# Token dispatch in a state-space and mixture-of-experts kernel: counts by a masked scan and two matmuls, two expert blocks begun ahead of the last count, the second block table in four parts

## The reference

```python
gate_logits = einsum('bsd,ed->bse', x, gate_w) + gate_b + expert_bias     # 8 experts
top_idx = argmax(gate_logits, axis=-1)
for e in range(8):
    mask = (top_idx == e)[..., None]
    h = relu(einsum('bsd,df->bsf', x, w1[e]) + b1[e])                      # 128 -> 512
    y = einsum('bsf,fd->bsd', h, w2[e]) + b2[e]                            # 512 -> 128
    out = out + mask * y
x = layernorm(x + out)
```

## Time and profile before

| | us |
|---|---|
| median of 3 runs (280.63 to 283.34) | 281.16 |
| the profiled execution's own time | 283.39 |
| its span, first to last instruction | 281.7 |
| PE busy in it | 248.6 |
| mixer, up to the first transpose of the quads | 144.4 |
| quad stage, up to the first transpose of a block | 51.4 |
| block stage and tail | 85.9 |

### The profile page before, as it was taken

How to read it: one execution, slowest core, us unless ns; L and a number is a source line. 1 busy time by engine, 2 the same in 40 slices (tenths; PEclk the granted TensorE clock), 3 DMA queues, 4 the chain that set the end, 5 groups by cost and what they waited for, 6 DMA issues and landing times.

```text
span 281.7 us, 8736 instructions
## 1 busy us (share of the span) xinstructions
PE 248.6 (88%) x2801; PEld 220.3 (78%) x2801; DVE 174.6 (62%) x553; ACT 188.3 (67%) x522; POOL 125.5 (45%) x144
## 2 busy tenths in 40 slices
PE   4799999999977878699988999593999999999970
PEld 1588888888866555467678999492999999999970
DVE  2789984999435433255542575847656766666672
ACT  5969999927988656477846565311577777777740
POOL 5000000400018867499900477746524545554455
PEclk9999999999997999799999999868699999999996
DMA  6639777500199999899337231136677777877510
GB/s 218 186 119 360 294 276 282 219 0 0 40 316 302 311 287 306 237 236 329 90 109 303 72 116 56 58 77 197 145 201 202 226 195 214 220 191 209 158 37 5
DMA packets 54243, 52.12 MB, mean 185 GB/s; under 512 B 4399, under 2 KB 42801, under 8 KB 54082
## 3 DMA queue, kind: packets, MB, share of 16 engines
q1 hardware_dynamic: 50930, 45.60, 54.7%
q0 software_dynamic: 2272, 4.27, 4.3%
q10 hardware_dynamic: 1008, 1.84, 2.0%
HBM read 38.14 MB, written 14.00 MB: 185 GB/s over the span
## 4 chain that ended last, share of the span: by engine, by line
PE 85%; DVE 5%; issue 4%; ACT 2%; POOL 1%; DMA 1%; SPq 0%; DVEq 0%; ACTq 0%; POOLq 0%
PE banks L1188 20%; PE banks L1357 13%; PE banks L1368 11%; PE banks L1240 6%; PE banks L1191 5%; PE banks L1306 5%; PE banks L1250 4%; PE banks L1233 4%; PE banks L1254 4%; PE banks L1304 3%; PE banks L1289 2%; PE banks L1323 2%; PE banks L1347 2%; PE banks L1198 1%; POOL out L554 1%
## 5 line engine op out<-in xcount | busy, mean ns | idle before, releaser
L1188 PE MATMUL banks<-Wx,XT 128*128 128x256 f32 x256 | 62.7, 389 | 1.4 <-DVE Wx L797 1.4
L747 ACT ACTIVATE Z<-banks,BR 128x128 f32<-128x128 f32 x156 | 44.7, 367 | 21.0 <-PE banks L1357 20.9
L1188 PEld LDWEIGHTS banks<-Wx,XT 128*128 128x128 f32 x256 | 49.9, 196 | 10.3 <-DVE Wx L797 3.0
L554 POOL DMA_INDIRECT out<-X x39 | 38.3, 983 | 39.3 <-DVE X L1144 28.5
L485 POOL TENSOR_TENSOR Wx<-BR,RE 128x384 f32 (+1 forms) x32 | 47.8, 1518 | 9.4 <-PE banks L1233 9.2
L1357 PE MATMUL banks<-Z 128*128 128x128 f32 x312 | 43.6, 285 | 0.3 <-ACT Z L731 0.3
L538 POOL DMA_INDIRECT dispatched_rows<-TR,CR x32 | 31.2, 974 | 26.4 <-issue 22.1
L1368 PE MATMUL banks<-BR,Z 128*128 x312 | 40.9, 275 | 0.0
L1357 PEld LDWEIGHTS banks<-Z 128*128 128x128 f32 x312 | 40.2, 201 | 0.7 <-issue 0.7
L1368 PEld LDWEIGHTS banks<-BR,Z 128*128 128x128 f32 x312 | 37.8, 192 | 0.0
L978 DVE TENSOR_TENSOR X<-banks,Z 128x256 f32 (+1 forms) x32 | 13.6, 424 | 26.2 <-PE banks L1254 26.2
(11 more groups left out here) (202 smaller groups left out, 468.2 us busy)
## 6 DMA issues: line engine op xcount, KB each, us to landing
TR<-kernel_rows SPq DMA_DIRECT2D x32, 512.0 KB, 6.2
Z<-w SPq DMA_DIRECT2D x35, 256.0 KB
dispatched_rows<-TR SPq DMA_DIRECT2D x3, 2310.0 KB, 8.7
X<-dispatched_rows SPq DMA_DIRECT2D x39, 66.0 KB, 2.5
XT<-hidden_t SPq DMA_DIRECT2D x10, 256.0 KB, 3.2
RE<-decay_and_turns SPq DMA_DIRECT2D x2, 1024.0 KB, 7.4
BR<-w SPq DMA_DIRECT2D x1, 2048.0 KB, 7.7
dispatched_rows<-TR SPq DMA_DIRECT2D x1, 1848.0 KB, 7.8
```

The costliest lines, as they stand in the source:

```text
L554: pool.indirect_dma_start(out_rows, bass.IndirectOffsetOnAxis(XS[:, n % ROWS_RING, TOKEN_COL:TOKEN_COL + 1].bitcast(U32), 0), F[:, slot, : ...
L747: last = nc.scalar.activation(HT[:, slot, c * P:c * P + P], bank[n % 4][:, c * P:c * P + P], ACT.Relu, bias=B1[:, bass.ds(experts[n % 4] * ...
L1188: mm(bank[X_BANKS[k]][:, j * CHAN:(j + 1) * CHAN], XT[:, slot, at:at + CHUNK], Wx[:, tap, :], start=(tap == 0), stop=(tap == TAPS - 1))
```

## The change

It touches the quad stage, the tables and the first steps of the block stage:

- **Count.** `OH` becomes expert by five (four tiles and a zero). DVE runs a new `tensor_tensor_scan` over its 40 columns, multiplied by the mask `carry` (0 at the first of each expert, 1 elsewhere), which gives inclusive running sums over the tiles (`upto`, `s_upto`). PE has two products of 40 columns: `before`, now -1 for the rows at or behind and 0 elsewhere, with `OH`, and `ones` with `upto`. The fifth column of each expert is its total, so `places` loses a reduction.
- **PE's order.** In step 2 `count` stands ahead of `output_projection`. The last count (quad 7) stands behind the transposes of blocks 0 and 1 and `up` of block 0. These wait for quad 6's `s_sq` and `s_x1`; the banks are dealt anew for it (`UP_BANKS`, `SLOT_BANKS`, `DOWN_BANKS`). The other waits of the block stage stand behind the count, that for the last `s_pl` in step 3.
- **First weights.** `stage_weights` of blocks 0 to 3 moves from ACT's queue to SP's, behind the first `s_be2`.
- **Tables.** The same arithmetic in a few operations less, in four functions; the first table calls them in a row. The second is spread: one part behind `moments` of each of blocks 0 to 3.
- **Constants.** POOL sets three more small areas (`s_oc`) ahead of `s_rconst`; DVE waits for both and computes `full_from` (two operations) ahead of its copy of the first transposes.

```diff
 # SP
             sp.wait_ge(s_be2, 1)
+            experts = table_values(sp, bexp, 0, EXPERTS - 1)
+            for n in range(STAGE_RING):
+                stage_weights(sp, n, experts[n])
             sp.wait_ge(s_first, 1)
...
 # DVE, choose and places
-                    tt(OH[:, slot, :, :], first, each_expert(top[:, 1, :]), ALU.is_equal).then_inc(s_oh, 1)
+                    tt(hot(slot), first, each_expert(top[:, 1, :]), ALU.is_equal).then_inc(s_oh, 1)
+                    dve.wait_ge(s_oh, n + 1)
+                    nc.vector.tensor_tensor_scan(upto[:, slot, :], carry, OH[:, slot, :, :].rearrange("p e k -> p (e k)"), 0.0,
+                                                 ALU.mult, ALU.add).then_inc(s_upto, 1)
...
-                    nc.vector.tensor_reduce(total, bank[6 + slot][:, 32:64].rearrange("p (k e) -> p e k", k=4), AX.X, ALU.add)\
-                      .then_inc(s_pl, 1)
...
 # DVE, tables
+            def blocks_by_expert(quads, at):
+                if at:
+                    done(ts(taken, c(3)[:, 0:EXPERTS], -1.0, float(EARLY_BLOCKS), ALU.mult, ALU.add))
+                    done(stt(taken, taken, 0.0, blocks, ALU.max, ALU.min))
+                dve.wait_ge(s_pl, quads * 4)
+                done(stt(blocks, free_row, 1.0 / P, full_from[:, 1 if at else 0, :], ALU.mult, ALU.subtract))
...
+                ts(bexp[:, at:end], bexpf[:, 0:count], EXPERTS - 1.0, None, ALU.min).then_inc(s_be2, 1)
...
-            block_table(QUADS, EARLY_BLOCKS, BLOCKS + 1)
...
                     moments(new)
+                    if new == 0:
+                        blocks_by_expert(QUADS, EARLY_BLOCKS)
+                    elif new == 1:
+                        experts_of_blocks(EARLY_BLOCKS, BLOCKS + 1)
+                    elif new == 2:
+                        rows_of_kinds(EARLY_BLOCKS, BLOCKS + 1)
+                    elif new == 3:
+                        rows_of_blocks(EARLY_BLOCKS, BLOCKS + 1)
...
 # PE
-                    mm(counted[:, 0:32], before[:, :], flat(hot), start=True, stop=False)
-                    for m in range(1, 4):
-                        mm(counted[:, m * EXPERTS:32], ones[:, :], flat(hot[:, 0:4 - m, :]), start=False, stop=(m == 3))
-                    mm(counted[:, 32:64], ones[:, :], flat(hot), start=True, stop=True).then_inc(s_cp, 1)
+                    mm(counted, before[:, :], OH[:, slot, :, :].rearrange("p e k -> p (e k)"), start=True, stop=False)
+                    pe.wait_ge(s_upto, n + 1)
+                    mm(counted, ones[:, :], upto[:, slot, :], start=False, stop=True).then_inc(s_cp, 1)
...
-            for s in range(QUADS + 2):
+            for s in range(QUADS + 1):
                 if s != 1:
                     transpose_gated(s)
+                if s == 2:
+                    count(s)
                 output_projection(s)
...
+            pe.wait_ge(s_sq, (QUADS - 1) * 4)
+            pe.wait_ge(s_x1, QUADS - 1)
+            for step in range(AHEAD):
+                transpose_slots(step)
+                up(step)
+            count(QUADS + 1)
```

More of the change, by code:

```diff
@@ L60 @@
 EARLY = 14
+UP_BANKS, SLOT_BANKS, DOWN_BANKS = (0, 1, 4, 5), (2, 3), (6, 7)
+AHEAD = 2
 ROWS_RING, OUT_RING, STAGE_RING, DEEP = 12, 8, 4, 4
@@ L1053, in places @@
-                    tt(place, place, OH[:, slot, :, :], ALU.mult).then_inc(s_pl, 1)
-                    tt(free_row, free_row, total, ALU.add).then_inc(s_pl, 1)
-                    dve.wait_ge(s_pl, n * 5 + 4)
+                    wait_past(dve, s_pl, n * 4)
+                    counted = bank[6 + slot][:, 0:40].rearrange("p (e k) -> p k e", e=EXPERTS)
+                    tt(place, counted[:, 0:4, :], free_row.unsqueeze(1).to_broadcast([P, 4, EXPERTS]), ALU.add).then_inc(s_pl, 1)
+                    dve.wait_ge(s_pl, n * 4 + 1)
@@ L1056, in places @@
+                    tt(place, place, hot(slot), ALU.mult).then_inc(s_pl, 1)
+                    tt(free_row, free_row, counted[:, 4, :], ALU.add).then_inc(s_pl, 1)
+                    dve.wait_ge(s_pl, n * 4 + 3)
                     nc.vector.tensor_reduce(posf, place, AX.X, ALU.add).then_inc(s_pl, 1)
-                    dve.wait_ge(s_pl, n * 5 + 5)
+                    dve.wait_ge(s_pl, n * 4 + 4)
                     stt(pos[:, batch, :], posf, -1.0, posf, ALU.mult, ALU.max).then_inc(s_pos, 1)
-            def block_table(quads, at, end):
-                c = lambda i: cnt[:, i, :]
-                blocks, taken = c(1)[:, 0:EXPERTS], c(5)[:, 0:EXPERTS]
+            c = lambda i: cnt[:, i, :]
@@ L1065, in block_table, with kinds_of @@
+            blocks, taken = c(1)[:, 0:EXPERTS], c(5)[:, 0:EXPERTS]
+            def kinds_of(at, end):
                 count = end - at
                 shape = [P, count, KINDS]
[L1067 to L1072, removed]
@@ L1073, in block_table @@
-                done(tt(c(0)[:, 0:EXPERTS], free_row, ebase, ALU.subtract))
-                done(ts(blocks, c(0)[:, 0:EXPERTS], 1.0 / P, spare_rows / P - 0.5 + 0.5 / P, ALU.mult, ALU.add))
+                return (count, lambda a: a.unsqueeze(1).to_broadcast(shape), brow[:, 0:count].unsqueeze(2).to_broadcast(shape),
+                        passed[:, 0:count, :], begun[:, 0:count, :], block_rows[:, 0:count, :])
+            def blocks_by_expert(quads, at):
[4 more added lines that the diff above has]
+                done(stt(blocks, free_row, 1.0 / P, full_from[:, 1 if at else 0, :], ALU.mult, ALU.subtract))
@@ L1371, in down @@
                     last.then_inc(s_dn, 1)
+            pe.wait_ge(s_sq, (QUADS - 1) * 4)
[4 more added lines that the diff above has]
+            count(QUADS + 1)
+            pe.wait_ge(s_ew, 32)
+            pe.wait_ge(s_be2, 1)
+            pe.wait_ge(s_sq, QUADS * 4)
+            pe.wait_ge(s_x1, QUADS)
             experts = ()
-            for step in range(BLOCKS + 3):
+            for step in range(AHEAD, BLOCKS + 3):
+                if step == 3:
+                    pe.wait_ge(s_pl, QUADS * 4)
                 transpose_slots(step)
```

89 lines of the change are left out of this document (47 added, 42 removed).

## The result

The changed kernel takes 273.81 us (median of 4 runs, 271.17 to 274.2), the kernel before beside it 280.89: 7.1 us less, ratio 0.9712 with a 95% interval of 0.9669 to 0.9756. The forecast was 273.3. Both profiled executions are slower than their medians: 283.39 before, 274.2 after.

What follows compares the result with a forecast made beforehand. PE was taken as full in quads and blocks, with loose time before the first down product. Moving that 9.2 us earlier, less 1.3 for the second table, gave 281.16 - 7.9 = 273.3 us (272.0 to 274.8).

Steps and rivals of the forecast that it cites:

- Counts: PE's counts in quad steps 3 to 6: 0.6 us saved per step, 2.4 in all, full steps of 4.2 us.
- Step 2 and constants: Quad 0's count ahead of the output product: 0.1 us lost; added constants ahead of DVE's copy: 0.2 us.
- First table and quads 5 to 7: Places and first table 4.3 us instead of 5.2; quad 5's choice at 179.5 instead of 182.50; PE's wait about 2.5.
- When a block can begin: Start of the blocks, bound by POOL's dispatches: slot loads at 184.3, 0.9 us earlier; first transpose at 186.5, 9.3 earlier.
- To the first down: From the first block transpose to first down: 7.2 us at half clock, 4.7 at full; first down at 192.9, 9.2 earlier.
- First weights: First weights issued from SP's queue, covered by 8 us of idle: cost 0; on ACT's queue they would become late.
- The second table: Spread over blocks on DVE: residuals of blocks 1 to 4 lag 0.7, 1.8, 2.1, 3.4 us; PE loses 1.3.
- Block 12: SP's load of block 12, behind the second table: landed at 217.9, in time with 1.5 us to spare.
- full clock: Rival: full clock from the slots on, and DVE's lag fits: 271.1 us; chance 0.14.
- the late slots: Rival: slots come late (4.0 us to land, POOL slower), all at half clock: 275.0 us; chance 0.08.
- a wait of 3 us: Rival: blocks wait 3 us for DVE or ACT instead of 1.3, or run partly half clock: 275 to 276.6; chance 0.16.
- the lag: Rival: DVE, ACT's root and PE wait on each other, setting the block loop's pace: 284 us or more; chance 0.03.

## Why the prediction was right

**What bounds the kernel** was read rightly: the change moved the first down product, and the blocks behind it kept their 1.893 us, apart from DVE's table. One reading in it was short: the stretch of 68.74 us ends 2.0 us ahead of the last down instruction (272.8), which is why the table above has 70.7.

**Counts.** 0.6 saved per step was forecast, steps of 4.2. The steps are 4.03 to 4.10, 0.7 saved: the two products take 0.37 (157.13 to 157.50), 0.09 per instruction, a little under the shorter end of the bounds. The scan took 0.24 for 0.25.

**Step 2 and constants** cost nothing (0.3 was allowed). Step 3 starts 11.5 behind the mark, after 11.6 before. The added constants are covered: the first output product, which waits for DVE's copy, starts 2.05 behind the mark (144.06), after 2.07 before.

**First table and quads 5 to 7.** Quad 5's choice is 38.1 behind the mark before and 34.3 after, 3.8 earlier; 3.0 was forecast, the difference being the two terms above. The wait of 2.5 came out as said. The output product took 4.44 us (177.17 to 181.61), the half-clock end of the bounds.

**When a block can begin.** The forecast had the first load 0.9 earlier and the first transpose 9.3. Measured 0.9 and 9.3. The sum was right, but one step in it was not. The forecast let POOL start 2.6 earlier and then wait for quad 1. POOL started only 0.8 earlier, 3.3 us behind the places instead of 1.0, and did not wait after: quad 1's dispatch at 160.43 is 18.4 behind the mark, where the forecast, in the same measure, had 18.4 as well. Two bounds lay at nearly the same place: quad 1's count was over at 157.5, and with the 2.36 us of the forecast its dispatch could have gone at 159.9, half a microsecond earlier than it did. That the number came out is luck here: the slots were bound by POOL's late start and its pace, not by the count of quad 1.

**To the first down.** 7.2 us at half clock was forecast, 4.7 at full. It was 7.25 (184.00 to 191.25), all at half clock. I had taken a middle, 9.2 earlier in all; it was 8.4 (57.66 - 49.24). That is the mis-sized term: 0.8. Here the granted clock is 0.50 over 6.43 us behind two waits of 2.50 and 1.74 us, and 1.00 when the same waits are filled. The level is not sure even so: behind waits of 2.42 and 2.56 us the run with half of the table ahead had its first up product at full clock, and 5.8 us from the first transpose to the first down. By the rule of the Trainium skill, page TensorE: Matmul & The Clock Gate (Part 1), that the throttled state is the default and activity releases it, the forecast would have been 0.8 higher; the two traces of the changed kernel agree with it (0.50 from the first up to the first down), that of the run with half of the table ahead only in part.

**First weights.** Put at 0 with SP and as the late one with ACT, without a price. The run shows 2.4 to 2.8 for ACT.

**The second table.** Lags 0.7, 1.8, 2.1, 3.4 forecast; 1.0, 1.9, 2.1, 3.6 measured, and a PE wait of 1.27 at down 6 for 1.3. In the stretch from the first to the last down it costs 1.5 to 1.6. The cover of 2.4 was right too: at a lag of 3.6 PE waited 1.27, which leaves 2.3 to 2.4, and at 1.9, with the whole table ahead, it did not wait. What the forecast did not draw from its own numbers is that the table fits better ahead of the blocks: it wrote that spreading hides nothing more and only lets the first down come before it, but not that DVE would idle 3.8 us just there.

**Block 12** was loaded at 204.00, its transpose came at 208.92. It fitted.

**The sum**: -9.2 + 1.3 = -7.9 forecast, -8.4 + 1.6 = -6.8 in the two traces, -7.1 in the medians and -8.1 in the means. So the total is nearer to the forecast than its terms were in the traces: both the clock and the table came out on the costly side. The rivals: full clock and the late slots did not come in that execution, nor did a wait of 3 us; the lag did not lock in.

## What to carry to other kernels

When a stage is moved forward, list every input of its first step with its own earliest time. Here the rows' dispatch, not the count that was made shorter, set the start; with counts of the old length PE would have set it, and the first down would have come 2.3 to 2.7 later. A transfer that had been hidden would have become late if it had not moved too. Before work that is hidden in an engine's idle time is spread over the busy stage behind it, compare the lag that each part gives with the buffers' cover: here spreading cost 1.5 to 1.6 us, and leaving all or half of it in the idle time cost none. Compare two profiles from a mark just ahead of the change, not by their spans; 2.4 of 9.3 us here lay ahead of it.

## What was not expected of the hardware

- Behind waits of 2.50 and 1.74 us, with work between them, TensorE ran at half clock for 6.4 us; in another execution, behind 2.42 and 2.56 us, for about half as long. Filling the waits with useless products held the clock at 1.00 and brought the first down 2.3 us forward, although the products occupy the queue in front of the critical ones.
- POOL's first scatter comes 3.3 to 3.5 us behind the first places in all 13 traces of the changed kernel and its variants, and 1.04 before. In each of the 13, instruction transfers fall into this gap, and none in that of the kernel before: in the transfers of the changed kernel from 151.86 to 155.13

```profile
q8 instruction: 1, 0.02, 2.3%
q14 instruction: 1, 0.01, 0.6%
```

  The first column is transfers, the second MB, the third the share of the 16 engines. That POOL waits for its code there is a guess: transfer and gap stand together, and 48 empty instructions ahead of it moved neither.
- The same kernel took 281 us on one chip and 293 on another. In traces of its variants on the second, ACT, DVE and PE stop for up to 8 us with no releaser that the profile can name.
